# A graph-attention layer on one core: normalising x on GpSimd instead of ScalarE, and a front with six row buffers

## The reference, cut to what matters

```python
h = jnp.maximum(_layernorm(x, axis=-1), 0.0)              # x: 4096 x 256, h likewise
neib_att = jnp.tanh(neigh @ Wn1 + bn1) @ Wn2 + bn2        # 4096 x 32
value = neigh @ Wv + bv                                   # 4096 x 128
x_att = jnp.tanh(h @ Wx1 + bx1) @ Wx2 + bx2
ws = leaky_relu(x_att @ neib_att.T, 0.01)                 # 4096 x 4096
ws = softmax(where(adj > 0, ws, -9e15), axis=1)
out = x + concatenate([h @ Wfx + bfx, ws @ value], axis=1)
```

## Time and profile before

| what | value |
|---|---|
| median of three runs | 505.74 us (505.12 to 506.63) |
| the profiled execution: its time, and its span from first to last instruction | 505.33 us, 503.5 us |
| PE busy | 474.3 us (94%) |
| ACT busy | 434.8 us (86%) |
| DVE busy | 425.3 us (84%) |
| POOL busy | 213.5 us (42%) |
| granted TensorE clock, mean over the span | 0.999 |
| HBM read | 80.81 MB |

### The profile page before, as it was taken

How to read it: one execution, slowest core, us unless ns; L and a number is a source line. 1 busy time by engine, 2 the same in 40 slices (tenths; PEclk the granted TensorE clock), 3 DMA queues, 4 the chain that set the end, 5 groups by cost and what they waited for, 6 DMA issues and landing times.

```text
span 503.5 us, 9162 instructions
## 1 busy us (share of the span) xinstructions
PE 474.3 (94%) x2964; PEld 368.3 (73%) x3007; DVE 425.3 (84%) x824; ACT 434.8 (86%) x625; POOL 213.5 (42%) x341
## 2 busy tenths in 40 slices
PE   6888898999999999999999999999999999998996
PEld 4767666776777677777777778777777787766884
DVE  1449898999898999999898989899998989994664
ACT  1675999999999899989999899989999999987552
POOL 1441042445644673457445663476445534540100
PEclk9999999999999999999999999999999999999999
DMA  8995475464567435755566356754564556500100
GB/s 232 269 217 105 102 127 87 78 141 77 85 120 172 77 59 100 159 111 86 78 133 142 67 85 126 168 83 62 97 142 81 85 105 125 85 1 1 43 2 21
DMA packets 38191, 52.04 MB, mean 103 GB/s; under 512 B 4096, under 2 KB 29952, under 8 KB 38144
## 3 DMA queue, kind: packets, MB, share of 16 engines
q0 software_dynamic: 9216, 33.56, 40.0%
q1 hardware_dynamic: 27856, 17.83, 11.8%
q10 hardware_dynamic: 1072, 0.07, 0.1%
HBM read 80.81 MB, written 4.19 MB: 169 GB/s over the span
## 4 chain that ended last, share of the span: by engine, by line
PE 64%; ACT 12%; issue 9%; DVE 8%; DMA 4%; POOL 2%; ACTq 1%; DVEq 0%; SPq 0%
PE ps_turned L924 17%; PE ps_scores L901 10%; PE ps_product L943 8%; PE ps_product L945 8%; PE ps_product L944 8%; PE ps_scores L900 4%; ACT pt_hi L516 3%; ACT scores L555 3%; ACT scores L543 3%; DVE scores L692 3%; PE ps_product L870 2%; DVE pt_lo L674 2%; DMA b<-in_L_gnn_bx 2%; POOL scores L419 2%; DMA x_left<-in_x 1%
## 5 line engine op out<-in xcount | busy, mean ns | idle before, releaser
L674 DVE TENSOR_TENSOR pt_lo<-ps_turned,pt_hi 128x512 fp32r<-128x512 f32 x256 | 172.9, 686 | 39.6 <-ACT pt_hi L516 20.6
L419 POOL TENSOR_TENSOR scores<-scores,mask 128x512 f32<-128x512 f32 x109 | 126.9, 1165 | 171.8 <-ACT scores L543 171.7
L516 ACT ACTIVATE pt_hi<-ps_turned 128x512 fp32r<-128x512 f32 x256 | 156.1, 610 | 37.7 <-PE ps_turned L924 37.2
L924 PE MATMUL ps_turned<-ident,scores 128*128 128x128 f32 x1024 | 154.6, 273 | 2.5 <-DVE pt_lo L674 2.3
L924 PEld LDWEIGHTS ps_turned<-ident,scores 128*128 128x128 f32 x1024 | 123.8, 140 | 44.2 <-DVE pt_lo L674 15.1
L543 ACT ACTIVATE scores<-ps_scores 128x1024 f32<-128x1024 f32 x128 | 132.4, 1035 | 5.7 <-PE ps_scores L901 5.7
L555 ACT ACTIVATE scores<-scores,neg_top 128x2048 f32<-128x2048 f32 x64 | 129.4, 2022 | 0.0
L692 DVE CUSTOM_DVE_ANT_0 scores<-ps_scores,scores,top 128x1024 f32<-128x1024 f32 x96 | 122.5, 1276 | 3.3 <-ACT scores L543 3.0
L943 PE MATMUL ps_product<-pt_hi,v_hi 128*128 128x512 f32 x256 | 122.1, 477 | 0.2 <-DVE pt_lo L674 0.2
L901 PE MATMUL ps_scores<-neib,xs 128*128 128x512 f32 x256 | 108.8, 502 | 3.7 <-DVE top L692 1.3
L945 PE MATMUL ps_product<-pt_lo,v_hi 128*128 128x512 f32 x256 | 101.4, 396 | 0.0
(11 more groups left out here) (76 smaller groups left out, 367.1 us busy)
## 6 DMA issues: line engine op xcount, KB each, us to landing
adj_in<-in_adj POOLq DMA_DIRECT2D x62, 512.0 KB, 5.4
scores<-in_L_gnn_neigh SPq DMA_DIRECT2D x8, 512.0 KB, 6.6
x_rows<-in_x SPq DMA_DIRECT2D x8, 512.0 KB, 3.7
x_left<-in_x SPq DMA_DIRECT2D x8, 256.0 KB, 6.7
x_right<-in_x SPq DMA_DIRECT2D x8, 256.0 KB, 2.9
out_h<-x_left SPq DMA_DIRECT2D x8, 256.0 KB, 3.4
out_h<-x_right SPq DMA_DIRECT2D x8, 256.0 KB, 3.4
scores<-in_adj POOLq DMA_DIRECT2D x2, 512.0 KB, 9.9
```

The lines of the kernel that those rows point to most:

```text
L419: pool.tensor_tensor(half, half, mask[:, s % MASK_RING, BANK:CHUNK], ALU.add).then_inc(masked, 1)
L516: act.activation(pt_hi[:, (2 * b + u) % HI_RING], pt[:, u], ACT.Copy).then_inc(hi_done, 1)
L674: dve.tensor_tensor(pt_lo[:, u], pt[:, u], pt_hi[:, (2 * b + u) % HI_RING].bitcast(FP32), ALU.subtract).then_inc(lo_done, 1)
L924: last = pe.transpose(pt[:, u, i * P:(i + 1) * P], scores[:, parity * TILES + i, n * P:(n + 1) * P], ident[:, :])
```

## The change

**The normalisation** moves from ACT to POOL. `x_normalise` is now one `tensor_scalar` a tile of 128x256, (x - mean) * rstd, in place, at steps 1, 2, 4 and 4. The rectifier is applied later: `x_turned_copy` on ACT uses Relu in place of Copy on the turned x. The operations for `mean_neg` and `shift` go: 14 small POOL operations a group instead of 16.

**POOL's step** is reordered: the adjacency load, then the right sums, the left sums, then the mask add, then the Newton rounds and the normalisation. The sums are at steps 12 and 13 (right) and 12 and 14 (left), the Newton rounds at 12, 13 and twice 15.

**Other orders.** ACT does `power` ahead of the side work of its step, DVE does `close` ahead of the x work, the value layers start at step 0 instead of 1, and the first left half is written out at step 3 instead of 1.

**The front.** Six row buffers; `x_ahead` is gone, and the second group of x comes into its usual place once the first is turned, so its statistics are taken by DVE in the last front step. Wn2 and Wx2 come by one DMA each into `w2_raw`, and DVE spreads them (`spread_w2`, four copies each). The biases each have a semaphore, and four of the six small loads that ACT issued go to SP's queue, between the row loads. ACT runs one tanh on a column ahead of its first copy. PE starts with 15 transposes of the identity instead of 12 and has 6, 6 and 4 more inside front steps 0, 1 and 2 (`FILL`). The first x is turned in front step 4 instead of 5. The four first adjacency loads wait for later rows, two of them for the second group of x.

```diff
-ROWS_RING = 5
+ROWS_RING = 6
-TURN_X = 5
-PACE = (4, 5, 6, 7)
+TURN_X = 4
+FILL = (6, 6, 4, 0, 0, 0, 0, 0)
-X_LOAD = -8
+X_LOAD = -6
-X_RSTD = (-3, -2, -1, -1)
-X_NORM = (0, 1, 2, 4)
+X_RSTD = (-4, -3, -1, -1)
+X_NORM = (1, 2, 4, 4)
-X_LEFT_LOAD, X_SUM = 11, (10, 13)
-X_RIGHT = 7
-V_START, V_STRIDE = 1, 2
+X_LEFT_LOAD, X_SUM = 13, (12, 14)
+X_RIGHT = 8
+V_START, V_STRIDE = 0, 2
+LEFT_0 = 3
-WARM_UP = 12
+WARM_UP = 15
...
             load_neigh(0)
             load_neigh(1)
             load_x_rows(0)
+            load_w2(0, wn2)
             load_neigh(2)
-            sp.wait_ge(cleared, 2)
-            load_w2(0, w2_n, wn2)
+            load_bias(b2[:, 0:1], bn2, b2_in[0])
             load_neigh(3)
+            load_w1(1, w1_x, wx1)
             load_neigh(4)
-            load_w2(1, w2_x, wx2)
-            sp.dma_start(x_ahead, x_tiles[:, TILES:2 * TILES, :]).then_inc(x_ahead_in, 16)
+            load_bias(b1[:, 1:2], bx1, b1_in[1])
+            load_w2(1, wx2)
+            load_bias(b2[:, 1:2], bx2, b2_in[1])
+            load_neigh(5)
...
+            def x_normalise(e, i):
+                pool.wait_ge(newton, NEWTON_OPS * (e + 1))
+                pool.sem_inc(pool_joined, 1)
+                pool.tensor_scalar(x_rows[:, i, :], x_rows[:, i, :], mean_var[:, i, 0:1], rstd[:, i:i + 1],
+                                   ALU.subtract, ALU.mult).then_inc(x_normed, 1)
...
-            def x_normalise(e, i):
-                act.wait_ge(x_rows_in, 16 * (e + 1))
-                act.wait_ge(newton, NEWTON_OPS * (e + 1))
-                act.activation(x_rows[:, i, :], x_rows[:, i, :], ACT.Relu, bias=shift[:, i:i + 1],
-                               scale=rstd[:, i:i + 1]).then_inc(x_normed, 1)
...
-                act.activation(x_rows_t[:, k, :], bank, ACT.Copy).then_inc(x_turned_out, 1)
+                act.activation(x_rows_t[:, k, :], bank, ACT.Relu).then_inc(x_turned_out, 1)
...
+            act.wait_ge(made, 1)
+            act.activation(agg[:, 0:1], ident[:, 0:1], ACT.Tanh)
             turned_copy(0)
-            act.wait_ge(b1_in, B1_IN)
+            act.wait_ge(b1_in[0], 16)
...
+                if e == NEIGH_GROUPS - 1:
+                    for i in range(TILES):
+                        x_stats(1, i)
+                    x_aggr(1)
```

150 lines of the change are left out of this document (79 added, 71 removed).

## The result

The changed kernel takes 501.44 us (median of 4 runs, 500.86 to 501.64), the kernel before 506.19 us on the same chip: ratio 0.9908, 95% interval 0.9887 to 0.9929. It is faster by 0.9%, about 4.7 us; 13.4 us were forecast (492.3), and the time lies above the range of 487 to 500.

A forecast was written before the change was run, and what follows sets the result against it. Prediction: PE, ACT and DVE near their limit, PE first, with stalls behind DVE's masks; 505.33 - 4.5 + 0.4 - 9.0 - 0.3 = 491.9 us profiled, 492.3 as median, range 487 to 500.

The forecast's parts named there:

- The steady term, -9.0 us: Steady groups: lighter ACT and sums moved off DVE's masks cut periods from 54.3 to 52.65 us, -9.0 in all.
- a bound of 52.0: Steady groups: PE's matmuls alone, 16 plain steps plus the x work and a narrow layer, make 52.0 us a period.
- The operation's price: POOL's normalisation of one tile: 0.5 us, between 0.20 (the 128x4 operation) and 0.74 (the two-input sum).
- Rival A: Shared path, 22%: each POOL normalisation holds a DVE mask for its whole length, periods fall only 0.7 us, median 497.7.
- Rival C: POOL becomes the bound, 4%: slow normalisations delay mask adds, deciding from 1.7 us each; 510.5 us at 2 us each.
- Steps 0 to 19, +0.4 us: First score to step 19: +1.8 statistics, +0.5 late load, -1.5 ACT's normalisations and absorption, -0.4 adjacency wait.
- "-0.4": Steps 0 to 19: the adjacency wait of 0.86 us goes, about half of which reached ACT, saving 0.4 us.
- The +1.8 us for DVE's statistics: Start of steps 0 to 19: second x's statistics (1.41 us) and aggregation (0.38) delay DVE's first leak by 1.8 us.
- The ninth chunk's load: Steps 0 to 19: POOL issues it 11.7 us after the first score, landing at 17.6; DVE waits 1.5 us.
- Rival B: First steps starve, 14%: the ninth or fifth chunk lands late behind the second x, +3 us, 495.3 us total.
- The front, -4.5 us: Before the first score: earlier turning (-2.6) and two vanished waits (-1.7), taken as -4.5; first score near 33.8 us.
- the fast pace: Front: added transposes keep PE busy, so a front step takes 2.54 us from the start.

The follow-up runs named there:

- norm_tiny: Changed kernel with POOL's normalisation cut to the first 4 of 256 columns, the others left unnormalised; 500.40 us, ratio 0.9888.
- v_late: Changed kernel with the value layers starting at step 1 and the first left half stored at step 1, as before; 503.36 us, ratio 0.9949.
- load_first: Changed kernel with the ninth chunk's adjacency load right behind the first four, ahead of Newton's rounds, and right sums moved to step 4; 501.20 us, ratio 0.9909.
- sums_old: Changed kernel with POOL's old order within a step and the sums at their old steps, normalisation still on POOL; 506.93 us, ratio 1.0037.
- best2: load_first with rows_turn5's edits added; 500.11 us, ratio 0.9895.
- rows_turn5: Changed kernel with the third neighbour rows loaded ahead of the first x block and x turned at front step 5; 499.77 us, ratio 0.9893.

## Why the prediction was wrong

Right in its signs: faster, the gain in the steady groups the largest, a loss in steps 0 to 19, the end at nothing. Wrong by 9 us in size (13.4 forecast, 4.7 measured), in three terms: 3.1 us too much in the steady groups, 3.6 too little loss in steps 0 to 19, 1.6 too much in the front.

**The steady term, -9.0 us, measured -5.9.** The mechanism was right: the sums' place is worth 0.8 to 1.1 us a group, and the visible waits before steps 12 and 14 of the earlier trace rows are gone. The step that failed is "I take the periods from 54.3 to 52.65", built on "DVE, ACT and POOL all keep a margin, and PE's stalls shrink" and a bound of 52.0 from single rows. The periods came out at 53.0 to 53.4. The plain steps and the pieces were priced rightly; what the sum lacks is 1.1 us in steps 5, 9 and 15, of which steps 9 and 15 were already that long in the sixth period of the kernel before, the one that the forecast meant to undercut by 0.3. The saving on ACT was counted too fully: 2.0 us a group taken off ACT moved the group by 0.39.

**The operation's price**, 0.5 with bounds 0.20 and 0.74, measured 1.26. The upper bound was a guess about kinds ("with one input less"): an operation that no row shows is not bounded by a neighbour of another kind. It did little harm in the steady part: norm_tiny gains 0.15 us a group, and nothing over steps 0 to 19 as a whole. The Trainium skill (GPSIMD Engine Reference, Engine selection) calls one-input work near line rate and two-input work about twice as slow as on VectorE; between the two kinds the runs show the reverse order, 0.92 to 1.26 us against 0.60 to 0.74, so here the measurement decides. The estimate of 0.35 to 0.70 us made from it missed as well.

**Rival A**, the shared path, didn't come as described: the masks' mean fell from 511 to 473 ns (447 in norm_tiny). A normalisation lengthens a mask that begins inside it by 0.1 to 0.2 us and doesn't hold it for its own 1.26 us, so the rule of a lock for a whole instruction, which the prediction quotes, fits the mask beside the left sum (0.42 + 0.74 = 1.16, measured 1.21, though that mask's row begins before the sum's) and not these. Its time, 497.7, was nearer only by chance. **Rival C** has the right mechanism, and its threshold of 1.7 us lies between the two lengths that were run: 0.15 us a group at 1.26 us (its formula makes 0.9), 2.3 us a group at 2.4 (its formula makes 4.3), so POOL has more slack than I gave it.

**Steps 0 to 19, +0.4 us, measured +4.0.** The table of starts adds them up: 0.9 us at step 1, 0.6 from step 1 to 4, 2.5 from 4 to 14, -0.5 from 14 to 19, and 0.5 by which the two marks on PE lie further apart than the two rises on ACT. The first term that failed is one that wasn't there: the value layers' start at step 0 was listed in the change and put at nothing without a reason. It costs the 0.9 us at step 1, which is shown, and the chain through `v_lo` makes it the likely cause of the 1.0 us at steps 12 to 14. The second is "-0.4", the wait for adjacency that was to go: DVE waits for adjacency four times in this stretch, 2.98 us in all, where it waited 0.86 us once. The third is the late normalised x, priced at nothing, for which PE waits 0.63 us. The +1.8 us for DVE's statistics was a real row of 1.41 us in a place where PE was 0.9 us late anyway; v_late has them and loses nothing at step 1. The ninth chunk's load was forecast to the tenth of a microsecond and DVE's wait for it nearly (1.5, measured 1.03). **Rival B**, starving for adjacency, is thereby there in part, with at most 1 us to its name in load_first and not its 3; its time, 495.3, was not met.

**The front, -4.5 us, measured -2.9.** The landing (12.14 against 11.9) and the order were right. "With PE kept busy from the start by the added transposes I take the fast pace from there" failed in the profiled execution: behind 3.18 us of idle time the granted clock fell to 1.2 GHz for 3 us. In the two executions in which it stayed up and nothing else in the front was changed, the first score came at 33.94 (v_late) and 34.04 (sums_old), forecast 33.8. So the term is right for those; where the clock fell behind the wait for the third rows, the first score came at 35.3 to 36.7.

## What to carry to other kernels

Price every line of a change, the harmless constants most of all: here moving a small layer by one step cost as much as the new operation was thought to. When three engines are near their limit, set the steps of the best period that the trace already has side by side with the sum of their pieces, one by one: the steps that are longer than their pieces there will be so after the change, unless it touches what holds them. And a late transfer is a finding, not yet a cost: move it alone before counting on it.

## What was not expected of the hardware

- GpSimd's `tensor_scalar` on 128x256 fp32: 0.92 us (one constant), 1.07 (one column), 1.13 (two constants), 1.26 (two columns), and 0.45 for 128x4 with two columns; its product of two tensors with one spread from a column 0.605.
- A bf16 mask on VectorE (0.42 us alone) takes 1.21 us when GpSimd's two-input sum of 128x256 runs beside it, and 0.52 to 0.65 us inside GpSimd's `tensor_scalar` of the same tile, which itself lasts 1.26 us.
- In 14 of the kernels the third rows land at the same time (12.09 to 12.32 us) behind about 3 us of idle PE. In 10 of them the clock granted between 13 and 16 us was 0.50 to 0.64, in 4 it was 1.00; with the rows first (idle 1.0 to 2.1 us) it fell there in 1 of 4, behind the 2.08 us of best2, and one of the others, rows_turn5, ran at 0.95 throughout. Each kernel was profiled once, so this is a spread over executions. A forecast should carry both outcomes. In eight of the ten the same eight transposes take 1.47 to 1.97 us instead of the 1.09 that v_late shows here; in the other two the clock fell behind them:

```profile
12.19 1.09 PE L796 MATMUL ps_turned<-ident,scores 128*128 128x128 f32 x8 [2.93 <-DMA scores<-in_L_gnn_neigh]
```
